# A decoder layer on one core: keys split inside PSUM by ScalarE and TensorE, and expert blocks computed with the weights stationary

## What is computed

```python
x = x + attn(layernorm(x))        # 16 heads of 64; every tensor truncated to multiples of 1/4096
x = x + xattn(layernorm(x), ctx)  # 16 heads of 8; keys = values = ctx, 4 x 1601 x 128, no projection; then relu(c @ wo.T + b)
x = x + ffn(layernorm(x))         # 8 experts, the best 2 per token
# ffn, per expert: z = (x @ W1 + b1) * (x @ W2 + b2)          W1, W2: 128 x 256
#                  o = silu(z @ Wg + bg) * (z @ Wl + bl)      Wg, Wl: 256 x 256
#                  y = o @ W3 + b3                            W3: 256 x 128
```

## Time and profile before

| | us |
|---|---|
| median of 3 runs | 750.12 |
| the profiled execution, its own time | 743.64 |
| its span | 741.9 |
| busy: TensorE, VectorE, ScalarE, Pool | 585.1, 531.5, 445.2, 185.7 |

### The profile page before, as it was taken

The page is one execution under the profiler, slowest core; times in us unless marked ns, Lnnn a source line. Parts: engine busy times, 40 slices in busy tenths (PEclk is TensorE's granted clock), DMA queues, the critical chain, the costliest instruction groups (busy, mean ns, idle before and its releaser), DMA issues.

```text
span 741.9 us, 13437 instructions
## 1 busy us (share of the span) xinstructions
PE 585.1 (79%) x4759; PEld 289.4 (39%) x4759; DVE 531.5 (72%) x896; ACT 445.2 (60%) x818; POOL 185.7 (25%) x234
## 2 busy tenths in 40 slices
PE   3775548888896856899999988889886875999981
PEld 2453335555554743333333333333331232444441
DVE  4466698899889987688888888788783245555541
ACT  3553338888889412687867876778674752334330
POOL 4325570000011233332115101500040044122222
PEclk9876679999999985999999999999996795999996
DMA  8332364724576802601090109000029001011103
GB/s 209 97 121 92 100 219 175 199 60 122 143 158 131 151 1 89 227 3 47 2 222 24 47 2 211 35 3 1 2 79 319 2 28 51 22 33 34 33 21 93
DMA packets 32667, 66.91 MB, mean 90 GB/s; under 512 B 4542, under 2 KB 21322, under 8 KB 32164
## 3 DMA queue, kind: packets, MB, share of 16 engines
q0 software_dynamic: 8960, 45.07, 22.9%
q1 hardware_dynamic: 22068, 20.31, 9.1%
q10 hardware_dynamic: 1584, 0.79, 0.4%
HBM read 46.45 MB, written 19.30 MB: 89 GB/s over the span
## 4 chain that ended last, share of the span: by engine, by line
PE 43%; DVE 32%; ACT 9%; issue 8%; DMA 5%; SPq 1%; DVEq 0%; ACTq 0%; POOLq 0%; POOL 0%
DVE smax L1647 12%; PE pair L1079 10%; DVE region_p L1550 6%; PE pair L1054 6%; PE pair L1233 5%; PE pair L1009 4%; PE pair L910 3%; PE pair L874 3%; DVE region_p L1520 3%; ACT region_p L1410 2%; ACT region_p L1329 2%; DVE region_p L1823 2%; PE pair L896 2%; DVE region_p L1553 2%; PE pair L963 1%
## 5 line engine op out<-in xcount | busy, mean ns | idle before, releaser
L1647 DVE TENSOR_REDUCE smax<-pair 128x2 f32<-128x1024 f32 x192 | 225.5, 1218 | 55.7 <-PE pair L1009 55.0
L1410 ACT ACTIVATE region_p<-pair 128x1024 f32<-128x1024 f32 (+3 forms) x277 | 217.5, 812 | 68.3 <-PE pair L1054 63.1
L910 PE MATMUL pair<-ident,region_p 128*128 128x128 f32 x256 | 39.3, 302 | 45.3 <-DVE region_p L1553 45.3
L1520 DVE SCALAR_TENSOR_TENSOR region_p<-region_p 128x1024 int16<-128x1024 int16 (+1 forms) x56 | 67.6, 1229 | 9.1 <-ACT region_p L1315 6.6
L1079 PE MATMUL pair<-region_p 128*32 128x256 f32 (+1 forms) x832 | 69.8, 410 | 0.5 <-ACT region_p L1417 0.4
L1079 PE MATMUL pair<-region_p,region_b 128*32 128x256 f32 (+1 forms) x832 | 66.5, 391 | 0.4 <-ACT region_p L1417 0.4
L1550 DVE TENSOR_SCALAR region_p<-region_p,rnorm 128x256 f32<-128x256 f32 x128 | 62.1, 548 | 1.1
L1054 PE MATMUL pair<-region_b,region_k 59*128 59x256 bf16 (+1 forms) x416 | 54.7, 273 | 8.2 <-ACT region_p L1410 4.0
L1009 PE MATMUL pair<-region_k,region_b 56*128 56x512 bf16 (+1 forms) x256 | 44.5, 365 | 16.8 <-DVE smax L1647 15.6
L910 PEld LDWEIGHTS pair<-ident,region_p 128*128 128x128 f32 x256 | 31.0, 154 | 59.9 <-DVE region_p L1553 59.2
L1329 ACT ACTIVATE region_p<-region_p 128x256 f32<-128x256 int16 x128 | 51.3, 409 | 0.0
(11 more groups left out here) (244 smaller groups left out, 968.3 us busy)
## 6 DMA issues: line engine op xcount, KB each, us to landing
kimg<-region_k SPq DMA_DIRECT2D x56, 200.1 KB
region_k<-kimg POOLq DMA_DIRECT2D x8, 1400.9 KB, 12.4
region_b<-in_mask_Bx1xSxS_ff POOLq DMA_DIRECT2D x12, 800.5 KB, 7.0
region_p<-in_mask_Bx1xSxS_ff POOLq DMA_DIRECT2D x4, 800.5 KB, 13.2
region_b<-in_ctx SPq DMA_DIRECT2D x4, 768.0 KB
region_k<-in_L_ffn_W POOLq DMA_DIRECT2D x3, 1024.0 KB, 8.4
xdisp<-region_x POOLq DMA_DIRECT2D x1, 2322.0 KB, 21.1
xdisp<-region_x POOLq DMA_DIRECT2D x1, 2257.5 KB, 18.4
```

What stands on the lines that cost most here:

```text
L910: last = pe.transpose(pair[1][:, c:c + 128], attn[:, b % 2, a:a + 128], ident[:, :])
L1410: act.activation(pT[0:rows, first // 3 % 2, k:k + size], home[0:rows, 0:size], ACT.Exp).then_inc(expt_made, 1)
L1520: return dve.scalar_tensor_tensor(out_, floor16, 0.0, floor16, ALU.is_lt, ALU.add)
L1647: last = dve.tensor_reduce(units[:, :, c // 3, c % 3], both, AX.X, ALU.max)
```

## The change

1. Keys. The batches come in the order 0, 2, 3, 1, each into a place of its own, and SP issues all four loads in the prologue, the first ahead of the small parameters and the other three behind them. A half's transposes stay in PSUM. ScalarE casts the half from PSUM to bfloat16 (part 0); TensorE subtracts that part in PSUM with a product by a bfloat16 matrix of minus one on the diagonal; ScalarE casts again (part 1), TensorE subtracts again, ScalarE casts the last time. Pool's `split` and ScalarE's `ctx_move` go. Halves 0 and 1 are done in the prologue in pair 1, halves 2 to 7 in head pairs 0 to 5, one each, in pair 2.
2. TensorE's and ScalarE's head pairs are written out instead of looped; VectorE keeps its loop. Pool moves the values of batch 0 early, loads the image of batch 0 during head pairs 4 and 5 and that of batch 1 behind the mask of batch 0, and stores the pads of the dispatch table in head pairs 2 and 3 instead of 6 and 7.
3. Experts. ScalarE copies the block's weights from the resident tables to a double buffer (`stage_up`: 512 columns; `stage_gl`: 1024 columns). TensorE uses 128 x 128 pieces of them as the stationary operand and the tokens or z as the moving operand of 128 columns, so that every result has features on partitions and needs no transpose. `zed_transposes`, `zed_move`, `ogl_transposes` and `ogl_move` go. A bias is now one value a partition, read by VectorE with a broadcast over the tokens; the biases are loaded once as 32 rows and transposed (`biases_T`).

The core of the diff:

```diff
+            def ctx_subtract(h, i):
+                k, first, size, home = half_of(h)
+                pe.wait_ge(cast_made, 3 * h + i + 1)
+                for c in range(0, size, 512):
+                    end = min(c + 512, size)
+                    last = pe.matmul(home[:, c:end], negb, kparts[:, k % 2, i, first + c:first + end],
+                                     start=False, stop=True, skip_group_check=True)
+                last.then_inc(ctx_sub, 1)
 # TensorE, head_pair(hp), half = hp + 2 for hp < 6
                     if b + 2 < B or not last:
                         dots(*batch_of(hp, b, 2))
+                    if half is not None and b == 2:
+                        ctx_transposes(half)
+                    if half is not None and b == 3:
+                        ctx_subtract(half, 0)
                     if b < 2 and not last:
                         project_qk(hp + 1, b)
                     if (b or not first) and (b != 2 or last):
                         attn_values(*batch_of(hp, b, -1))
+                    if half is not None and b == 3:
+                        ctx_subtract(half, 1)
                     attn_transposes(hp, b)
-                    if first and b:
-                        ctx_transposes(b, (2, 2))
 # ScalarE
+            def ctx_cast(h, i):
...
+                act.activation(kparts[:, k % 2, i, first:first + size], home[:, 0:size], ACT.Copy).then_inc(cast_made, 1)
                     if b or not first:
                         attn_move(*batch_of(hp, b, -1))
+                    if half is not None and b == 3:
+                        ctx_cast(half, 1)
                     if b == 2 and not last:
                         round_qkv(hp + 1, 2)
                     if b + 2 < B or not last:
                         round_dots(*batch_of(hp, b, 2))
                     if b < 2 and not last:
                         round_qkv(hp + 1, b)
-                    if first and b:
-                        ctx_move(b, (2, 2))
+                    if half is not None and b >= 2:
+                        ctx_cast(half, 0 if b == 2 else 2)
 # Pool
-            for k, b in enumerate(CTX_ORDER):
-                pool.wait_ge(ctxT_made, 2 * k + 2)
-                if k >= 2:
-                    pool.wait_ge(kimg_written[k % 2], 224)
-                split(kparts[:, k % 2, :, :], ctxT[:, k, :], ctxT[:, k, :], kparts_made)
 # TensorE, experts
-                pe.matmul(up_bank[j % 2], xblkT[:, j % 2, :], w12[:, bass.ds(expert[j] * (2 * FF), 2 * FF)],
-                          start=True, stop=True).then_inc(up_mm, 1)
+                for m in range(4):
+                    last = pe.matmul(up_bank[j % 2][:, m * 128:(m + 1) * 128],
+                                     staged[:, j % 2, m * 128:(m + 1) * 128],
+                                     xblkT[:, j % 2, :], start=True, stop=True)
...
+                for m in range(4):
+                    for f in range(2):
+                        last = pe.matmul(gl_bank[j % 2][:, m * 128:(m + 1) * 128],
+                                         staged[:, j % 2, (f + 1) * 2 * FF + m * 128:(f + 1) * 2 * FF + (m + 1) * 128],
+                                         zed[:, j % 2, f * 128:(f + 1) * 128], start=(f == 0), stop=(f == 1))
...
-                if j >= 2:
-                    ogl_transposes(j - 2)
...
-                if j < NBLK:
-                    zed_transposes(j)
 # ScalarE, experts: order of iteration j
+                    block_move(j + 1)
+                    stage_up(j + 1)
+                if j >= 2:
+                    y_move(j - 2)
                 if 1 <= j <= NBLK:
                     gate_silu(j - 1)
+                if j + 1 < NBLK:
+                    stage_gl(j + 1)
```

More of the change, by code:

```diff
@@ L553, in _ @@
             sp.dma_start(b3_sb[:, :], b3).then_inc(small_loaded, 16)
+            for k in range(1, B):
+                ctx_load(sp, CTX_ORDER[k], ctx_home[k], ctx_loaded[k])
             def weights_load(hp):
@@ L629, in _ @@
             pool.wait_ge(ident_made, 2)
+            pool.tensor_scalar(negb, ident[:, :], -1.0, None, ALU.mult).then_inc(ident_made, 1)
             pool.memset(ones, 1.0).then_inc(ones_made, 1)
             chain.step(pool.memset(v_aug[:, :, :], 1.0))
[L634 to L641, removed]
-                        pool.tensor_copy(parts[:, i, :], src).then_inc(signal, 1)
             def move_values(nat, home, signal):
@@ L705, in _ @@
             mask_load(0)
+            for k in range(2):
+                pool.wait_ge(kimg_written[k], 448)
+            for a in range(2):
+                keys_load(1, a)
             pool.dma_start(xdisp[:, D + 1:ROW].rearrange("(n p) c -> p (n c)", p=128), pad_index.bitcast(F32),
@@ L926, in _ @@
             weights_T(0)
+            ctx_subtract(0, 0)
             project_qk(0, 0)
-            pe.wait_ge(ctxT_made, 2)
+            ctx_subtract(0, 1)
             project_qk(0, 1)
+            pe.wait_ge(small_loaded, 16 * 7)
+            pe.transpose(pair[3][:, 512:640], xo[:, :], ident[:, :]).then_inc(small_T, 1)
+            ctx_transposes(1)
             project_v(0)
+            ctx_subtract(1, 0)
             dots(0, 0)
+            ctx_subtract(1, 1)
             dots(0, 1)
             def head_pair(hp):
-                first, last = (isinstance(hp, int) and hp == end for end in (0, HP - 1))
+                first, last = hp == 0, hp == HP - 1
+                half = hp + 2 if hp + 2 < 2 * B else None
                 for b in range(B):
@@ L965, in project_out @@
                 last.then_inc(proj_mm, 1)
-            repeat(pe, HP, head_pair)
+            for hp in range(HP):
+                head_pair(hp)
             attn_values(HP - 1, B - 1)
@@ L1215, in up @@
                 pe.wait_ge(xblkT_made, j + 1)
+                pe.wait_ge(wup_staged, j + 1)
                 wait(pe, z_made, j - 1)
[L1217 to L1226 removed]
@@ new lines, in up, with gate_linear @@
+                last.then_inc(up_mm, 1)
+            def gate_linear(j):
+                pe.wait_ge(wgl_staged, j + 1)
+                pe.wait_ge(z_made, j + 1)
+                wait(pe, glb_made, j - 1)
+                for m in range(4):
+                    for f in range(2):
+                        last = pe.matmul(gl_bank[j % 2][:, m * 128:(m + 1) * 128],
+                                         staged[:, j % 2, (f + 1) * 2 * FF + m * 128:(f + 1) * 2 * FF + (m + 1) * 128],
+                                         zed[:, j % 2, f * 128:(f + 1) * 128], start=(f == 0), stop=(f == 1))
@@ L1236, in gate_linear, with down @@
                 last.then_inc(gl_mm, 1)
-            def ogl_transposes(j):
+            def down(j):
                 pe.wait_ge(ogl_made, j + 1)
-                wait(pe, oglT_made, j)
-                for f in range(2):
-                    last = pe.transpose(oT_bank[:, f * 128:(f + 1) * 128], ogl[:, j % 2, f * 128:(f + 1) * 128], ident[:, :])
-                last.then_inc(ogl_T, 1)
-            def down(j):
-                pe.wait_ge(oglT_made, j + 1)
                 wait(pe, yblk_made, j)
```

278 lines of the change are left out of this document (149 added, 129 removed).

## The result

The changed kernel takes 719.59 us (median of four runs, 713.96 to 722.63) against 750.70 for the kernel before on the same chip: a ratio of 0.9577, 95% interval 0.9515 to 0.9638, or 4.2% faster. The forecast was 700.6 with a range of 689 to 716. The sign is right and 18 of the 49.5 us are missing. The profiled execution takes 713.96 us, its span is 712.2; against the 743.64 of the profiled execution before that is -29.7.

A forecast was written before the change was run, and what follows sets the result against it. Pool's key split was taken to hold VectorE in head pairs 0 and 1, and TensorE to bound expert blocks. Self-attention -33.9 and experts -15.6 sum to -49.5, taking 750.12 to 700.6 us, range 689 to 716.

The forecast's parts named there:

- Pairs 0 and 1: Self-attention's first head pairs: without Pool's split, pair 0 falls to 25.5 us (gain 28.5), pair 1 to 22.8 (gain 9.7).
- Rival F: Head pairs 0 and 1: something other than Pool's split holds VectorE, 38.2 us stay, 739 us; chance 0.03.
- Moved steps: Self-attention: reordered loads on SP's queue make nothing wait; Pool's moved pads and key loads net +0.2 us (-1 to +2).
- Casts: Head pairs 2 to 5: ScalarE's added key casts cost +4.6 us together, between nothing and 10.0.
- Rival B: Self-attention: ScalarE becomes the bound and every cast is paid, 710 us; chance 0.09.
- Prologue: Before the first exponential: added casts about cancel against earlier layer norm and fewer transposes, -0.5 us (-3 to +2).
- Cross-attention: Cross-attention stretch: taken as 0, with the wait for the maxima's DMA again near 7 us.
- D: Rival in cross-attention: the maxima's DMA no longer waits, -10.4 us, 690 us; chance 0.07.
- Experts: Expert blocks: 3.5 us each instead of 4.11, -12.8; start -1.9, tail -0.9; sum -15.6 us.
- C: Rival in the expert blocks: they stay at 4.11 us each, only start and tail gain, 713 us; chance 0.09.
- E: Rival in the expert blocks: weight loads stand bare, 6.8 us a block, 770 us; chance 0.02.
- Weight loads: Expert blocks on TensorE: full-height weight loads hide behind other products, 0.1175 us per instruction with load, against the skill's rule.

The follow-up runs named there:

- e7: The e1 kernel plus ten unused casts and ten subtractions of 1024 words on GpSimd during head pair 0 and part of pair 1: 712.47 us.
- e2: Changed kernel with the two pad stores issued beside the mask probes of head pairs 5 and 6 instead of 1 and 2: 719.30 us.
- e9: Changed kernel with the two pad stores issued early, from ScalarE's ninth cast on (near 50 us): 698.98 us.
- e1: Changed kernel with SP's weights loads of head pairs 4, 6 and 7 issued ahead of the image stores instead of behind them: 688.60 us.
- e10: Changed kernel with weights loads first, expert loads behind the maxima's copies, and pad stores early: 680.14 us.
- e5: The e1 kernel with ScalarE's copy of the transposed w_proj put back ahead of the first standard deviation: 692.67 us.
- e6: The e1 kernel with GpSimd's expert weight loads issued only after the maxima's copies of the last group but one have landed: 681.48 us.
- e4: The kernel before the change with only the expert blocks and biases changed: 727.54 us.

## Why the prediction was right and wrong

**Pairs 0 and 1: right, and better than forecast.** Pair 0 was put at 25.5 and takes 22.2. I had kept a low clock in its first steps; the clock stays full from the start, and 22.8 was the value that I had named for that (runs with the same pair 0 have it at 22.0 to 23.7). Pair 1 came at 22.5 for 22.8. L1591 (the old L1550) is at 39.4 us in all for 62.1. Rival F is refuted by the trace and, from the other side, by e7.

**Moved steps: the step that failed.** The prediction says "each load is wanted a head pair (22 us) after the release of its buffer, so nothing waits". The 22 us are right, but I set them against nothing, and put the wait at 0. The trace of before could have warned me. Its timeline of SP's queue has this row:

```profile
62.88 15.37 SPq L563 DMA_DIRECT2D kimg<-region_k  x14
```

14 issues are 15 us of the queue before the load is issued, which leaves 7 of the 22. The rest is how long the load takes once it is issued. Behind the stores that was 11.1 us (e2), 13.5 (e9) and, at pair 6, 12.8 to 13.5, so that the place comes to 22 to 30 us against the 23 that there are: a wait of 0 to 6. With the pads beside it, which I had named in the very next sentence, it was 30.3, and 9.4 MB moved from the first store to the end of the stall; so of the 22.6 us at least 16 took the pads as well. I followed the moved steps past each queue in order and didn't ask how long each queue is in time, nor what runs beside it. With the loads first (e1) pairs 2 to 5 take 31.5 us less, the whole of the miss of 18 and more.

**Casts: right.** +4.6 was the term; e1's pairs give +4.7, and e10's, without the pads beside them, +3.6. Rival B is refuted: ScalarE didn't become the bound.

**Prologue: right in kind, wrong in size.** -6.3 for -0.5, outside the -3 to +2 given. I let the five transposes and casts cancel against the earlier layer norm; e5 sizes the order at 2 to 3 us, and the rest is open.

**Cross-attention: right.** The stretch takes 0.5 us less where I put 0, less than it varies from one profiled execution to another. The wait for the maxima's DMA was forecast again near 7 and is 6.8 in the chain. D's mechanism, an end of that wait, didn't happen by the change; e6 makes it happen with one wait on GpSimd, and it is worth 7 to 8 us where D had 10.4, since the low clock behind it only moved.

**Experts: right, with two sizes off.** The block takes 3.25 for 3.5. In the middle of the stretch TensorE isn't idle at all:

```profile
641.00:689.00 48.00, 48.00 (x433) 48.00 (x432) 33.15 (x60) 35.73 (x76) 14.32 (x15) 1.00 0.15 41
```

So the 0.1 for waits was too much, and an instruction with its load takes 0.112 (3.25 / 29), not the 0.1175 of the earlier trace rows. That makes 21 x 0.86 = 18.1 for 12.8. Start and end gave 2.9 more where 2.8 stood. ScalarE is busy 35.73 / 14.8 = 2.4 us a block, for 2.8; the 0.4 put for a register load had no row, and the copy of 512 columns (L1505) has no idle time before it in this stretch. C and E are refuted. Against it stands a stretch that I put at nothing, from cross-attention to the first `up`: +4.6. Of it 3.2 is the longer gap with no releaser (2.90 in the chain before, 6.08 after); the rest I put down to the biases' transposes and copy and a lower clock, which no run takes apart. e4, with -18.8 in all, bears out the net of the two.

**Weight loads.** The rule that a weight load overlaps a running matmul only when its row group differs (the Trainium skill, "TensorE: Matmul & The Clock Gate", section "The mechanism"), by which full-height loads would stand bare, isn't borne out here: 29 instructions, each with a full-height load of its own, take 3.25 us, where rival E by that rule had 6.8.

## What to carry to other kernels

When a small load is moved behind large stores, count three things against the time at which its data are wanted: the issues ahead of it in its queue by their own duration, the bytes already in flight, and whatever other queues start in that window. Put what somebody waits for ahead of what nobody waits for, on every queue, and read the slack that is left and not only the waits: in e1 a load issued 2.2 us ahead of the pads still landed with them, 0.7 us before it was wanted. And when an experiment leaves the time unchanged, read its waits before calling the suspect innocent: e2 had removed a stall of 22.6 us and made one of 18.6.

## What the runs showed of the hardware

- A transfer of 3 KB takes 1.8 us alone and 6.8 with 3 MB issued 4 us ahead of it on another engine's queue. 192 KB issued behind 2.8 MB of stores took 11 to 13.5 us to land, and 30.3 with the pads beside them; issued 2.2 us ahead of pads of 2.3 MB they took 22.6, and 2.5 at 74.66 in e1, just ahead of the stores. The Trainium skill ("DMA: Bandwidth & Descriptors", section "Issuing engines are not separate DMA queues") says that transfers of all engines run on the same DMA engines and interleave; the runs agree, and show what the one that is waited for pays.
- The time that SP takes to issue 14 stores of 0.2 MB varies from 10.9 to 18.1 us: 14.4 to 18.1 where the pads or a key image started beside them, 10.9 to 15.0 where neither did. The two ranges overlap, so other traffic isn't the whole of it.
- The idle gap with no releaser on TensorE ahead of the last output transposes is 2.8 to 6.8 us. Holding GpSimd's scatter takes it from 6.0 to 2.8; what makes it differ between programs that all have the scatter there isn't shown.
- GpSimd's casts and subtractions of 1024 words, back to back, make a head pair that takes 23.6 us take 46.0.
